# Four buffers of normalized queries, and another order of GpSimd's work in a fused attention and coupling kernel

## The reference

```
x = x + xattn(layernorm(x), ctx, ctx, mask)        # 16 heads of 16
    u = q k^T * scale / sqrt(16);  logits = tanh(u) * exp(log_C);  masked keys -> -inf
    out = softmax(logits) v @ W_out.T
x = x + ffn(layernorm(x))
    gf = global_net(mean over tokens)              # 256 -> 128 -> 64 -> 1, gelu, sigmoid
    3 times: tf = coupling_net(out)                # 256 -> 256 -> 128 -> 64 -> 1, gelu, sigmoid
             coupling = 0.1 + range * (0.7 gf + 0.3 tf - 0.5) * 2
             out = out + coupling * twist(out)     # twist: quarters swapped, with signs
```

## Time and profile before

| | us |
|---|---|
| median of 3 runs (lowest, highest) | 1155.78 (1150.27, 1156.14) |
| the profiled execution | 1158.11 |
| its span, first to last instruction | 1156.2 |

### The profile page before, as it was taken

The page is one execution under the profiler, slowest core; times in us unless marked ns, Lnnn a source line. Parts: engine busy times, 40 slices in busy tenths (PEclk is TensorE's granted clock), DMA queues, the critical chain, the costliest instruction groups (busy, mean ns, idle before and its releaser), DMA issues.

```text
span 1156.2 us, 21972 instructions
## 1 busy us (share of the span) xinstructions
PE 998.3 (86%) x7260; PEld 536.9 (46%) x7260; DVE 793.2 (69%) x1738; ACT 928.4 (80%) x1153; POOL 584.0 (51%) x1117
## 2 busy tenths in 40 slices
PE   6889988899888998889888898888988889886894
PEld 4555435544455434554355543555435544453431
DVE  4876677757687485874858749577577757676285
ACT  5999679887798777987779877898679887794576
POOL 4577107871188602895048830688207871175303
PEclk8999999999999998999999999999999999997897
DMA  4110002210022100211002200122001220010002
GB/s 129 45 42 19 1 2 68 65 50 1 1 69 69 46 1 2 89 48 46 1 24 69 69 23 2 45 70 69 0 1 47 69 68 1 1 42 28 19 1 74
DMA packets 67281, 43.85 MB, mean 38 GB/s; under 512 B 42081, under 2 KB 50785, under 8 KB 67169
## 3 DMA queue, kind: packets, MB, share of 16 engines
q1 hardware_dynamic: 67168, 42.45, 13.0%
HBM read 25.51 MB, written 16.78 MB: 37 GB/s over the span
## 4 chain that ended last, share of the span: by engine, by line
PE 41%; DVE 21%; issue 14%; ACT 12%; POOL 10%; SPq 1%; DVEq 0%; DMA 0%; POOLq 0%; ACTq 0%
PE ps L1098 7%; PE ps L1143 7%; PE ps L1130 7%; PE ps L1156 5%; ACT probs L835 5%; PE ps L1067 4%; DVE move_u L727 4%; PE ps L1083 3%; ACT probs L841 3%; DVE coup L693 2%; DVE f_t L731 2%; PE ps L1186 2%; DVE move_u L706 2%; DVE move_v L708 2%; PE ps L1165 2%
## 5 line engine op out<-in xcount | busy, mean ns | idle before, releaser
L835 ACT ACTIVATE probs<-ps,u_scale 120x2048 f32<-120x2048 f32 x128 | 253.4, 1980 | 41.5 <-PE ps L1067 40.7
L841 ACT ACTIVATE probs<-probs,exp_bias,clip 120x2048 f32<-120x2048 f32 x128 | 269.5, 2106 | 0.1
L1156 PE MATMUL ps<-h,w 128*128 128x512 f32 x384 | 184.2, 605 | 14.0 <-ACT h L867 13.2
L1067 PE MATMUL ps<-q_t,k_t 32*120 32x256 f32 x2048 | 154.0, 416 | 32.0 <-ACT probs L835 31.2
L447 POOL TENSOR_TENSOR c<-tok_c 128x16 f32<-128x16 f32 x8 | 1.8, 222 | 330.7 <-issue 330.7
L637 DVE STREAM_TRANSPOSE o_t<-ps 128x512 f32<-128x512 f32 x128 | 91.2, 712 | 99.7 <-PE ps L1083 99.6
L1098 PE MATMUL ps<-wo_t,of_t 128*128 128x256 f32 x512 | 149.1, 417 | 8.5 <-DVE of_t L657 8.5
L1083 PE MATMUL ps<-probs,va 120*32 120x256 f32 x2048 | 140.2, 392 | 4.7 <-ACT probs L841 4.7
L1067 PEld LDWEIGHTS ps<-q_t,k_t 32*120 32x120 f32 x2048 | 96.1, 184 | 61.7 <-issue 56.3
L1098 PEld LDWEIGHTS ps<-wo_t,of_t 128*128 128x128 f32 x512 | 94.1, 204 | 44.6 <-issue 26.4
L498 POOL TENSOR_TENSOR f_hl<-f_t,f_hl 128x512 f16<-128x512 f32 x64 | 73.7, 1162 | 79.9 <-DVE f_hl L684 79.9
(11 more groups left out here) (129 smaller groups left out, 1849.6 us busy)
## 6 DMA issues: line engine op xcount, KB each, us to landing
xy<-in_x_dram SPq DMA_DIRECT2D x64, 256.0 KB, 2.9
out_dram<-xy SPq DMA_DIRECT2D x64, 256.0 KB, 2.0
cbuf<-in_ctx_dram SPq DMA_DIRECT2D x64, 120.0 KB, 2.7
tok_c<-coup SPq DMA_DIRECT2D x256, 0.5 KB, 2.0
move_v<-in_L_xattn_W_out_dram SPq DMA_DIRECT2D x1, 256.0 KB, 5.3
move_u<-in_L_ffn_cn_w_dram SPq DMA_DIRECT2D x1, 256.0 KB, 5.6
w<-in_L_ffn_cn_w_dram SPq DMA_DIRECT2D x1, 128.0 KB, 5.5
g<-in_L_ffn_gc_w_dram SPq DMA_DIRECT2D x1, 128.0 KB, 4.0
```

The source lines that it names most:

```text
L835: eng.activation(probs[:, b % 2, n * HALF:(n + 1) * HALF, :].rearrange("k h q -> k (h q)"), banks(SCORE_BANK, 4)[0:KEYS, :], ACT.Tanh, sca ...
L841: eng.activation(p, p, ACT.Exp, scale=clip[0:KEYS, 0:1], bias=exp_bias[:, b:b + 1]).then_inc(s_exp, 1)
L1067: last = eng.matmul(banks(SCORE_BANK + r)[0:KEYS, odd * S:(odd + 1) * S], k_t[rows, b % 2, odd, n, :], q_t[rows, b % 2, n, :], start=True, ...
L1156: last = eng.matmul(banks(bank), w2[:, k, :], h1[:, p % 2, k, :], start=(k == 0), stop=(k == EK - 1))
```

## The change

- `q_hat` and its statistics get a ring of four buffers (`QR`) in place of two.
- Which batch's queries are prepared is now given by `ahead_in_slot`: none at the positions 0, 1 and 4, batch `i+3` at 2 and 3, batch `i+2` at 5, 6 and 7. Three batches (before: one) are prepared in the ffn stage, two in front of the low halves of the third chunk and one between those of the third and the fourth. DVE's statistics follow the same list.
- `norm_2` and `query_hat` are cut in two. On POOL the small scale instructions now come first, and a part of `factors` stands between them and the pass that uses them. The scale of the queries stands in front of the x part, so it waits for DVE's statistics earlier in the slot.
- `HIGH_AT` goes from (3, 5) to (2, 4). `LOW_AT` stays.
- On SP the loads of a slot are issued in front of its store, and the load that stood in the slot behind an ffn stage is issued in that stage.

```diff
+    QR = 4
...
-        HIGH_AT = (3, 5)
+        HIGH_AT = (2, 4)
...
+        def ahead_in_slot(i):
+            if i < GROUP + LAG:
+                return i + 2 if i >= 0 else None
+            at = (i - LAG) % GROUP
+            return None if at in (0, 1, 4) else i + 3 if at < 4 else i + 2
+
+        def ahead_in_ffn(g):
+            early = g * GROUP + GROUP + LAG
+            return [b for b in range(early + 2, early + 5) if b < NB]
...
+                    for b in ahead_in_ffn(i)[2:]:
+                        load(b)
                     coupling_rows(i)
...
-                for b in late[:1]:
-                    store(b)
-                late = late[1:]
...
-                elif 0 <= i + 4 < NB and i >= -1:
+                elif 0 <= i + 4 < NB and i >= -1 and not after_ffn(i):
                     load(i + 4)
+                for b in late[:1]:
+                    store(b)
+                late = late[1:]
...
             def query_hat(b):
...
-                if b >= 2:
-                    eng.wait_ge(s_qtr, b - 1)
+                at = b % QR
+                if b >= QR:
+                    eng.wait_ge(s_qtr, b - QR + 1)
...
                 if 0 <= i - LAG < NB:
+                    norm_2_scale(i - LAG)
+                    if after_ffn(i):
+                        norm_2(i - LAG)
+                        coefficients(groups_before(i) - 1)
+                for b in late[:1]:
+                    twisted_part(b)
+                if 0 <= i - LAG < NB and not after_ffn(i):
                     norm_2(i - LAG)
-                if i == early:
-                    coefficients((i - LAG) // GROUP - 1)
+                if new is not None and 2 <= new < NB:
+                    query_scale(new)
                 for b in late[:1]:
-                    factors(b)
+                    x_part(b)
                 late = late[1:]
                 if 0 <= i + 1 < NB:
                     values(i + 1)
...
-                elif 2 <= i + 2 < NB and i != early:
-                    query_hat(i + 2)
+                if new is not None and 2 <= new < NB:
+                    query_hat(new)
```

More of the change, by code:

```diff
@@ L389, in _, with query_scale @@
             eng.wait_ge(s_pool0, 7)
-            def query_hat(b):
[L393 to L397, removed]
-                if b >= 2:
-                    eng.wait_ge(s_qtr, b - 1)
+            def query_scale(b):
+                at = b % QR
+                eng.wait_ge(s_mv, 2 * (b + 1))
+                eng.tensor_scalar(var1[:, at, :], mv1[:, at, :, 1], EPS, None, ALU.add).then_inc(s_var, 1)
+                eng.tensor_scalar(neg1[:, at, :], mv1[:, at, :, 0], -1.0, None, ALU.mult).then_inc(s_neg1, 1)
+                eng.wait_ge(s_var, b + 1)
+                eng.tensor_tensor(rstd1[:, at, :], var1[:, at, :], minus_half[:], ALU.pow).then_inc(s_rstd, 1)
+            def query_hat(b):
+                at = b % QR
+                if b >= QR:
+                    eng.wait_ge(s_qtr, b - QR + 1)
                 eng.wait_ge(s_rstd, b + 1)
@@ L422, in norm_2 @@
                 eng.tensor_tensor(rstd2[:, at, :], var2[:, b % 2, :], minus_half[:], ALU.pow).then_inc(s_rstd2, 1)
+            def norm_2(b):
+                at = b % XR
                 eng.wait_ge(s_neg2, b + 1)
@@ L485, in factors, with x_part @@
                                       ALU.add, ALU.mult).then_inc(s_tw, 1)
+            def x_part(b):
                 for t in range(TT):
@@ L499, in low_half @@
                    .then_inc(s_flo, 1)
-            early, late = None, []
+            late = []
             for kind, i in slots():
                 if kind == "ffn":
[L504 to L509, removed]
+                    ahead = ahead_in_ffn(i)
+                    for b in ahead[:2]:
+                        query_scale(b)
+                        query_hat(b)
+                    for k in range(EK):
+                        low_half(i, 2, k)
+                    for b in ahead[2:]:
+                        query_scale(b)
+                        query_hat(b)
+                    for k in range(EK):
+                        low_half(i, 3, k)
                     late = list(range(i * GROUP, (i + 1) * GROUP))
                     continue
-                if 0 <= i - LAG < NB:
+                new = ahead_in_slot(i)
+                if i == -2:
+                    for b in range(2):
+                        query_scale(b)
+                        query_hat(b)
+                if 0 <= i - LAG < NB:
+                    norm_2_scale(i - LAG)
[5 more added lines that the diff above has]
+                if 0 <= i - LAG < NB and not after_ffn(i):
                     norm_2(i - LAG)
-                if i == early:
-                    coefficients((i - LAG) // GROUP - 1)
+                if new is not None and 2 <= new < NB:
+                    query_scale(new)
                 for b in late[:1]:
-                    factors(b)
+                    x_part(b)
                 late = late[1:]
@@ L757, in end_combine @@
                    .then_inc(s_res, 1)
-            late, early = [], None
+            late = []
             for kind, i in slots():
@@ L763, in _ @@
                 if kind == "attention":
-                    new, nxt, here, old = i + 2, i + 1, i - 1, i - 2
+                    new, nxt, here, old = ahead_in_slot(i), i + 1, i - 1, i - 2
                     if i == -2:
@@ L775, in _ @@
                         keys_out(nxt)
-                    if 2 <= new < NB and i != early:
+                    if new is not None and 2 <= new < NB:
                         stats(new)
@@ L795, in _ @@
                 else:
-                    early = i * GROUP + GROUP + LAG
-                    if early + 2 < NB:
-                        stats(early + 2)
+                    ahead = ahead_in_ffn(i)
+                    for b in ahead[:2]:
+                        stats(b)
                     high_half(i, 2)
+                    for b in ahead[2:]:
+                        stats(b)
                     high_half(i, 3)
```

31 lines of the change are left out of this document (14 added, 17 removed).

## The result

The changed kernel is slower. Its median is 1168.4 us (1165.47 to 1171.42, 4 runs) against 1154.49 for the kernel before in the same comparison, a ratio of 1.0126 with a 95% interval of 1.0081 to 1.0171. I had forecast 1139.5 us and given 5% to slower. The profiled execution took 1171.42 us with a span of 1169.6, against 1158.11 and 1156.2.

The account below looks back on a forecast made before the run. Slots were bound by ACT in the first group, DVE at positions 3 and 4, POOL at 5. Per group 2.36 + 1.0 - 0.95 = 2.4 us, six give 14.5, with the tail 16.5: 1155.8 to 1139.3, taken as 1139.5; range 1127 to 1151.

Parts of the forecast that it names:

- Position 5: Queries made two slots early and no low half waiting for its high half: 11.00 becomes 8.64, 2.36 us gained a group.
- The meeting of POOL and DVE: In the slots, low halves overlap DVE's two-operand instructions and stretch them: -0.95 us a group, bounds 0 and -3.3.
- the sure hit: At position 4 the low half overlaps `o_n`; up to 1.1 us a hit, counted as 0.65 a group.
- a near miss: At positions 3 and 5 the low half begins about when L741 ends; 0.3 us a group counted for the others than position 4.
- the lag: At position 4 POOL starts 2.1 us behind the moment at which DVE starts `combine`.
- The rival that was slower: Four low halves a group each meet a two-operand DVE instruction and position 7 keeps its stall: 1166 us, chance 0.05.
- the kept stall: Position 7 keeps its stall for queries and the low clock, 1.9 us a group.
- Position 7: Queries ready 1.5 us behind DVE's start of `combine`; half the stall's cost saved, 1.0 of 1.9 us a group.
- the ceiling: POOL never late: a group takes 134.86 us, saving 4.35, with 73.04 from position 7 to restart; as a rival 1127 us, chance 0.2.
- The ffn stage and the loads: Three query batches in the ffn stage and reordered loads fit in existing waits: cost 0, ffn stage bounded at -1 to 0.
- The last group: No queries prepared, no low half before the long `o_n`, last f_hat earlier: 2.0 us gained, bounds 0 and 3.5.

Follow-up runs that it names:

- the first experiment: The changed kernel with each low half of the slots moved behind the pass f_hat, in front of the queries' scale: 1137.25 us, 0.9863 of the kernel before.

## Why the prediction was wrong

*Position 5.* Right in mechanism. The stall of 1.84 us is gone, and 11.00 became 9.2 (9.19 in the second group), not the 8.6 to 8.8 that I had named as a sign. The 0.60 us of the high half of position 4 now falls there, as that of position 2 falls into position 3. I had left the two high halves' time at the positions 4 and 6, where it had been, which changes nothing in the sum.

*The meeting of POOL and DVE, the step that failed.* I had the mechanism and, for `combine`, its price, up to 1.1 us a hit (measured 0.96). I had the place wrong, and for `o_n` the price too. I put the sure hit at position 4, on `o_n`, and called the positions 3 and 5 "a near miss" for which I counted 0.3 us a group together with 0.65 for position 4. The runs showed the opposite. In the changed kernel position 4 has no hit, and 3 and 5 have one in each of the six groups, with 6 in four of them. I had the low half at 0.75 to 0.9 us behind `combine`; it begins 0.15 us behind it. Small errors of the same sign made that. Counted from the `combine` before (218.60), I had the queries' pass begin at 8.65 us and, stretched by `combine`, end at 10.0. It began at 8.47 and the low half followed at 9.52, since the values took 0.85 in place of 0.95 and the pass met `combine` for 0.2 us only. And `combine` itself came at 9.37 in place of 9.23, as `o_n` had taken 0.86. At position 4 a hit at 3 delays DVE and takes from POOL the lag I had computed with, so the low half ends just in front of `o_n` (216.99 against 217.11).

But the 0.65 us for position 4 would have been wrong even without that. By my own numbers `o_n` starts 0.35 us ahead of the low half. Where the runs show this, six times with the high halves back and six times with four small passes in front, `o_n` stays at 0.69 and the low half gets longer: POOL pays, not DVE. I had taken the price from the `o_n` of 2.12 us at 1049.24 without looking at when its low half began, which is 0.41 us behind it:

```profile
1049.65 1.16 POOL L498 TENSOR_TENSOR f_hl<-f_t,f_hl 128x512 f16<-128x512 f32 x1
```

That `o_n` is one of two exceptions, told in the last section. The low half's operands are a float32 and a float16 one, not two float32 as I wrote.

A near miss worked out to 0.1 us was priced as a small mean, 0.3 us a group. But the slots repeat almost exactly, so it is nearly one event: at positions 3 and 5 it hit in all six groups, at position 6 in four. With the measured hits (15.3 us in six groups are 2.6 a group) in place of my 0.95, and the 0.9 at position 7 kept, my own sum gives 4.35 - 2.6 - 0.9 = 0.9 us gained a group. Most of the rest, down to the 2.4 lost, is the next point.

*The clock behind the hits.* Not in the sum. I had charged the lower clock to the stalls for queries alone. A hit makes PE wait 1.63 us for the query copy, and at position 4 the clock fell in five of six groups (11.35 against 9.8). Between 172 and 1022 us it fell 14 times in the changed kernel, eleven of them behind a hit and three at position 1. In the same stretch it fell 11 times in the kernel before, ten of them at the twelve stalls for queries, and twice in the first experiment. The stalls and their falls went, and the hits brought about as many new ones. In the first experiment four groups have no fall and take 135.6 us each. The changed kernel's six take 6.1 more each, 36.4 in all. Of these, 15.3 are the 16 hits. The other 21 are 1.5 for each of the 14 falls, which is also what the fall costs at position 4 (11.35 less 9.83).

*The rival that was slower* was this mechanism, with its condition of four hits a group and the kept stall, at 1166 us and 5%. Neither part of the condition held: there were two or three hits a group, and the stall was gone. These were enough, since they bring their own falls of the clock. Its mechanism and sign were right. That its 1166 us lies near the measured 1168.4 is luck. The chance was too small for a case of which I had written that three positions lie within 0.3 us of it.

*Position 7.* The queries are not late in the changed kernel, as DVE is later. The first experiment shows the forecast wait, 1.53 us against the 1.5 I had worked out. Half of 1.9 us was too little for the gain: that kernel has 73.29 us to the next restart in every group, against the 73.04 of the ceiling.

*The ffn stage and the loads.* Right. It is 72.9 us from the last tanh to the restart in the first group, where no fall of the clock lies in it. The third chunk's low halves begin at 255.37, where I had about 255, and PE reads them from 259.80:

```profile
255.37 2.27 POOL L525 TENSOR_TENSOR f_hl<-f_t,f_hl 128x512 f16<-128x512 f32 x2
```

The order of loads and store within a slot has no effect that shows.

*The last group.* Forecast 2.0, measured 2.2 us shorter. The long `o_n` is gone, and the last f_hat reaches PE 1.05 us earlier, counted from the group's start. What each part is worth was not measured.

*What stays open.* Why the clock falls at some equal waits and not at others. The length of the wait does not decide it. Waits of 1.53 us at position 7 all went without a fall, waits of 1.63 at position 4 brought one in five of six groups, and in the kernel with four small passes only one of five waits of 2.14 at position 7 was followed by a fall. The wide spread of that kernel goes with the clock: its five runs of 1142 to 1145.4 us have a mean granted clock of 0.978 to 0.982, its four of 1151.3 to 1153 one of 0.969 to 0.971.

## What to carry to other kernels

A wait that looks like waste can be what keeps two engines apart. Before removing one, ask what the released instruction will now stand beside, and look there for the longest cases of that pair in the old trace: here one row out of 56 gave the price of the mistake. For each such pair, ask which of the two starts first, since that settles which engine pays. In a loop that repeats, a near miss is not a small cost with a small chance. Work out its margin, and if that is under the error of the working, give the whole case, hits in every turn, the weight of a coin.

When an instruction that can hold up a neighbour engine has no tight deadline in its slot, put it where the neighbour reads PSUM, works with one operand or waits, not at the slot's end by default. That was worth 31 us.

## What the runs showed of the hardware that was not expected

- POOL's two-operand pass (128x512, float32 and float16 in, 1.16 us) and DVE's two-operand float32 instructions hardly run together, and nearly always the first to start wins. Where the pass was ahead of the first instruction of `combine`, this one ended 0.27 to 0.29 us behind the pass: it took 1.41 us with the pass 0.03 ahead, 1.24 with 0.20, 1.04 with 0.40, 0.88 with 0.55 and 0.51 when only 0.2 us of the pass was left. Where DVE's was under way, the pass got longer: 1.33 us beside the first `combine` instruction, and 1.18 to 1.64 when it began 0.54 to 0.07 us behind `o_n`, always ending 1.01 to 1.04 us behind it. This is what the Trainium skill ("SBUF — State Buffer", section "SBUF: two separate sides") describes as an exclusive lock. The traces agree for this pair, with two exceptions in the last group, one in the kernel before and one in that with the high halves back. There `o_n` began 0.41 and 0.22 us ahead of the low half and still took 2.12 and 1.93 us, to 0.55 us behind the low half's end. The x part was under way on POOL when it began. Why it lost is open.
- One-operand passes do not behave so. The pass of 1.49 us stretched DVE's 0.42 to 0.83 and itself to 1.66. A queries' pair of 1.10 us stretched it to 0.61 and itself to 1.49, six times in the first experiment. The values, 0.87 us long, leave `o_n` at 0.69 when they are 0.4 us ahead, and make it 0.86 when they are 0.09 us ahead. By the skill's rule DVE would have been stopped in each case.
- Four passes of 128x2 took 1.08 us on POOL and two took 0.71, where I had reckoned with 0.2 us each.
